# One accumulating DMA in place of four matrix products: the softmax denominators of a fused attention and feed-forward kernel

## The reference, cut to what matters

```python
def _L0_xattn_ref(q, k, v):                      # q = layernorm(x), k = v = ctx
    qh = q.reshape(b * h, d // h, m)             # 8 heads of 32 rows, m = 512
    kh = k.reshape(b * h, d // h, -1)
    vh = v.reshape(b * h, c // h, -1)
    qk = jnp.einsum('bdm,bdn->bmn', qh, kh) * scale
    sm = jax.nn.softmax(qk, axis=-1)             # over n = 512
    ret = jnp.einsum('bmn,bcn->bcm', sm, vh)
x = x + _L0_xattn_ref(_layernorm(x), ctx_2048, ctx_2048)
x = x + _L0_ffn_ref(_layernorm(x), W1, W2)       # quantised activations and weights, silu
```

## Time and profile before

| | |
|---|---|
| median of 3 runs | 783.78 us (780.02 to 784.09) |
| span of the profiled execution, first to last instruction | 780.7 us |
| instructions | 13868 |
| DMA traffic | 76.66 MB, mean 98 GB/s |
| mean granted PE clock | 0.987 of full speed |

### The profile page before, as it was taken

One profiled execution on the slowest core, in us unless ns is written; L12 is line 12 of the kernel. 1 busy time (PEld: TensorE's weight loads), 2 busy tenths in 40 slices (PEclk: granted clock), 3 DMA queues, 4 the chain that ended last, 5 costly groups with the idle time before them and its releaser, 6 DMA issues.

```text
span 780.7 us, 13868 instructions
## 1 busy us (share of the span) xinstructions
PE 718.7 (92%) x4324; PEld 280.2 (36%) x4324; DVE 693.9 (89%) x1588; ACT 634.8 (81%) x1017; POOL 630.5 (81%) x627
## 2 busy tenths in 40 slices
PE   0578699999999999999999999999999999999984
PEld 0112243333444444333344444333334344433322
DVE  2779999999999999999999999999999999997552
ACT  5486788888888898888888889888888888888852
POOL 3764778888889888888888998888888889877761
PEclk9999699999999999999999999999999999999998
DMA  8673213444333443344433334333443334330100
GB/s 293 167 197 111 55 43 107 109 110 109 98 92 84 109 99 78 96 109 109 109 101 92 85 105 100 81 92 109 110 109 103 94 86 101 82 82 25 46 28 13
DMA packets 53960, 76.66 MB, mean 98 GB/s; under 512 B 7808, under 2 KB 32384, under 8 KB 52864
## 3 DMA queue, kind: packets, MB, share of 16 engines
q1 hardware_dynamic: 53888, 75.79, 37.0%
HBM read 41.94 MB, written 8.39 MB: 64 GB/s over the span
## 4 chain that ended last, share of the span: by engine, by line
PE 83%; DVE 8%; DMA 3%; issue 2%; ACT 2%; SPq 1%; POOL 1%; POOLq 0%; ACTq 0%; DVEq 0%
PE pv L912 15%; PE mxp L902 15%; PE st L892 14%; PE bank_b L943 14%; PE dn L921 7%; PE bank_a L972 7%; PE bank_b L972 7%; DVE mx L727 4%; PE bank_a L931 3%; DMA late<-w 1%; DMA qs<-ql 1%; DMA qs<-qh 1%; ACT probs L585 1%; DVE late L796 1%; PE bank_a L954 1%
## 5 line engine op out<-in xcount | busy, mean ns | idle before, releaser
L585 ACT ACTIVATE probs<-st,sm 128x512 f32<-128x512 f32 x512 | 336.6, 687 | 52.7 <-PE st L892 26.9
L503 POOL TENSOR_TENSOR sums<-probs 128x512 f32<-128x512 f32 x256 | 333.3, 1321 | 20.8 <-ACT probs L585 20.8
L727 DVE TENSOR_REDUCE mx<-mxp 128x1 f32<-128x512 f32 x512 | 332.8, 676 | 18.5 <-PE mxp L902 14.9
L902 PE MATMUL mxp<-ks,qs 96*128 96x512 f16 x512 | 191.0, 403 | 18.2 <-DVE mx L727 12.4
L892 PE MATMUL st<-qs,ks 98*128 98x512 f16 x512 | 200.8, 394 | 1.7 <-ACT probs L585 1.6
L943 PE MATMUL bank_b<-w2t,late 128*128 128x512 f16 x512 | 128.1, 383 | 3.0 <-ACT late L615 3.0
L912 PE MATMUL pv<-probs,vt 128*32 128x512 f32 x1024 | 124.0, 602 | 0.0
L495 POOL TENSOR_TENSOR ql<-xn,qh 128x512 f16<-128x512 f32 x32 | 37.2, 1164 | 67.2 <-ACT qh L606 67.2
L892 PEld LDWEIGHTS st<-qs,ks 98*128 98x128 f16 x512 | 52.8, 103 | 99.3 <-ACT probs L585 40.1
L902 PEld LDWEIGHTS mxp<-ks,qs 96*128 96x128 f16 x512 | 50.7, 99 | 103.3 <-DVE mx L727 78.6
L801 DVE TENSOR_REDUCE hmx<-late 128x1 f32<-128x512 f32 x128 | 84.3, 679 | 1.1
(11 more groups left out here) (79 smaller groups left out, 896.6 us busy)
## 6 DMA issues: line engine op xcount, KB each, us to landing
cs<-ctx SPq DMA_DIRECT2D x32, 256.0 KB, 4.2
xs<-x SPq DMA_DIRECT2D x32, 256.0 KB, 4.0
late<-w SPq DMA_DIRECT2D x8, 1024.0 KB, 9.2
ks<-kh SPq DMA_DIRECT2D x64, 128.0 KB, 3.2
qs<-qh SPq DMA_DIRECT2D x64, 128.0 KB, 3.6
xr<-x SPq DMA_DIRECT2D x32, 256.0 KB, 3.0
vt<-values_t SPq DMA_DIRECT2D x32, 256.0 KB, 2.9
out<-late SPq DMA_DIRECT2D x32, 256.0 KB, 2.0
```

The source lines that it names most:

```text
L503: pool.tensor_tensor(sums[:, pair, h, :], probs[:, 2 * pair, h, :], probs[:, 2 * pair + 1, h, :], ALU.add).then_inc(sum_done, 1)
L585: act.activation(probs[:, c, h, :], st[u % 2][:, :], ACT.Exp, scale=sm1[:, r, ESC:ESC + 1]).then_inc(exp_done, 1)
L727: dve.reduce_max(mx[:, slot.ring(off), NC * h + c:NC * h + c + 1], mxp[m % 2][:, :], axis=AX.X).then_inc(max_done, 1)
L902: pe.matmul(mxp[m % 2][:, :], qs[0:3 * DH, r, h, c * P:(c + 1) * P], ks[0:3 * DH, r, h, :], start=True, stop=True).then_inc(mx_done, 1)
```

## The change

One step, `fold`, is added on POOL at unit 13: a DMA that adds all of `sums[:, 1]` into `sums[:, 0]` (float32, 128 partitions x 8 KB, 1 MB), issued by POOL once all eight sums are done, and it counts on a semaphore of its own when it has landed. `denominators` becomes one step of four products on `sums[:, 0]`, at 18 instead of two at 17, and waits for that semaphore. `invert` moves from 17 to 18. The first sum of pair 0 and of pair 1 now both wait for the one `denominators` of the tile before.

```diff
     sums=[4, 8, 9, 9, 10, 11, 11, 12],
-    denominators=[17, 17],
-    invert=[17],
+    fold=[13],
+    denominators=[18],
+    invert=[18],
...
-ORDER = {'pool': ['hidden_quantise', 'quantise', 'sums', 'xn', 'residual', 'rstd', 'ql', 'finish', 'rstd2', 'xn2',
+ORDER = {'pool': ['hidden_quantise', 'quantise', 'sums', 'fold', 'xn', 'residual', 'rstd', 'ql', 'finish', 'rstd2', 'xn2',
...
                 if h == 0:
-                    wait(pool, dn_done, slot, 2, off - 1, pair + 1)
+                    wait(pool, dn_done, slot, 1, off - 1, 1)
...
+            def fold(slot, off):
+
+                wait(pool, sum_done, slot, 2 * TH, off, 2 * TH)
+                pool.dma_start(sums[:, 0, :, :], sums[:, 1, :, :], accum_op=ALU.add).then_inc(sum_folded, 16)
...
-                wait(dve, dn_done, slot, 2, off, 2)
+                wait(dve, dn_done, slot, 1, off, 1)
...
-            def denominators(slot, off, pair):
-                wait(pe, sum_done, slot, 2 * TH, off, TH * (pair + 1))
-                if pair == 0:
-                    wait(pe, dn_spread, slot, 1, off - 1, 1)
+            def denominators(slot, off):
+                wait(pe, sum_folded, slot, 16, off, 16)
+                wait(pe, dn_spread, slot, 1, off - 1, 1)
                 for h in range(TH):
-                    last = pe.matmul(dn[DH * h:DH * (h + 1), :], ones[:, 0:DH], sums[:, pair, h, :],
-                                     start=(pair == 0), stop=(pair == 1), skip_group_check=True)
+                    last = pe.matmul(dn[DH * h:DH * (h + 1), :], ones[:, 0:DH], sums[:, 0, h, :],
+                                     start=True, stop=True, skip_group_check=True)
                 last.then_inc(dn_done, 1)
```

More of the change, by code:

```diff
@@ L315, in build @@
         sum_done = sem("sum_done")
+        sum_folded = sem("sum_folded")
         dn_done = sem("dn_done")
@@ L560, in run @@
                          "key_rsqrt": key_rsqrt, "xn": normalise, "ql": query_low, "finish": finish,
-                         "sums": pair_sum}
+                         "sums": pair_sum, "fold": fold}
                 for u in range(UNITS):
```

## The result

The changed kernel takes 1083.82 us (median of 4 runs, 1081.02 to 1085.94) against 783.75 us before: ratio 1.385, 95% interval 1.381 to 1.389. Forecast were 1140 us with a range of 950 to 1300.

A forecast was written before the change was run, and what follows sets the result against it. Bound: a closed loop from POOL's last sum through PE's denominators to the next tile's sums. Per tile 9.5 (landing) - 1.0 (removed) + 3.0 (clock) = +11.5 us; 31 intervals give +356 on 783.8, 1140 us, range 950 to 1300.

The forecast's parts named there:

- The closed loop: POOL's last sum, PE's denominators and the next tile's sums form a loop as long as the period, 0.4 us spare.
- D, the fold's landing: Time from POOL's last sum to the fold's landing, all added to the loop: 9.5 us, between 5.9 and 15.3.
- The prediction's own sign for the landing: The profile after would show a 1024 KB DMA from POOL with a landing of 8 to 10 us.
- What goes out of the loop: One product set (0.45 us) and work moved ahead of PE's wait (0.58 us) leave the loop: -1.0 us a tile.
- The first set costs and gives nothing: Dropping PE's first four denominator products, 0.9 us a tile, gains nothing: they covered a wait for unit 0's exponential.
- The clock: PE's stall halves its clock for about 6 us of work in each tile: +3.0 us, ends 0 and +6.5.
- The rival in which the clock stays: PE keeps full speed between stalls: landing still 9.5 us, +8.5 us a tile, 1047 us; chance 0.10.
- The rival of the plain rate: The fold lands like a plain transfer, in 5.9 us: 936 us, or 1029 with the clock loss; chance 0.22.
- The slow accumulate: The fold lands as late as the slowest weight load or later: 15.3 us, +17.3 a tile, 1320 us; chance 0.17.
- The other side: Not slower: the fold lands before PE reaches the denominators, below 1.1 us; at best 755 us, rather 780; chance 0.02.
- POOL's issue: Issuing the fold holds POOL 0.35 to 0.65 us, perhaps more; counted in the landing, later POOL work covered by idle time.

The follow-up runs named there:

- no_fold17: The changed kernel without the accumulating DMA (pair 1 missing from the denominators), its one set of denominator products and invert at 17 instead of 18; 779.9 us, ratio 0.997.
- plain_copy: The changed kernel with the same DMA as a plain copy, without the addition, so the denominators hold pair 1 alone; 984.1 us.
- keep_clock: The changed kernel with 26 extra PE products (about 5.5 us) ahead of the wait for the fold, to fill the stall; 1029.2 us, ratio 1.316.
- no_fold: The changed kernel without the accumulating DMA, one set of denominator products still at 18, pair 1 missing from them; 799.7 us, ratio 1.022.
- beside_store: The kernel before plus an accumulating DMA into a spare buffer no product reads, and SP's store moved from 56 to 61; 782.35 us, ratio 1.0005.
- beside: The kernel before, both product sets kept, plus the same accumulating DMA into a spare buffer that no product reads or waits for; 817.8 us, ratio 1.047.
- after_store: The changed kernel with SP's store moved from 56 to 61, so copies of kh and kl go ahead of it; 1081.7 us, ratio 1.383.

## Why the prediction was right, step by step

**The closed loop** was right, and it is what made the forecast. The sum by tiles: 300 us over 32 tiles are 9.4 us a tile (11.5 forecast, and over 31 intervals; the first tile's fold delays it too, 77.9 us for its first denominator against 69.5). One reading under it was wrong: the 57 waits of the earlier trace rows are the weight load's, not those of PE's matmuls, which never idled there. Before the change PE's own work held the period, with the loop over the last sum right behind it (`no_fold17`). The sum is not touched by this, since it counts from the last sum's end to the next scores as measured, 1.30 us, and the transfer makes that loop the longer one by far.

**D, the fold's landing** was sized too long: 7.5 us from the last sum in 24 tiles, 9.3 in the other eight, 8.0 on average against 9.5. The working that counted reading twice at the rate of 365 GB/s gave 7.7. I moved it up to 9.5 for SP's copies beside it and for the 9.2 us of the weight loads; but the usual landing is 7.1 to 7.2 us with these copies beside it, and they are the ones that suffer: `out` lands 5.7 us after its issue instead of 2.0. The prediction's own sign for the landing, 8 to 10 us, was missed with it, and the stall in front of `dn` is 6.5 us, not near 8. This is the term that accounts for most of the 56 us between forecast and result: 1.5 x 31 = 47 us. The clock's 0.5 x 31 = 16 us come on top, and the first tile's 8 us, which the sum did not have, go the other way. That D = 7.7 had been priced at 1084 us, the time measured, is partly luck: these two cancel most of each other.

The Trainium skill's rule that an add costs a second read through the same ring (page "Collectives: The Full Stack", section "The bandwidth ceiling: the fold count and why AG ≠ RS ≠ AR") fits: 0.645 against 0.33 us a packet. The runs show the halved rate; that the second read is its cause is the page's reason, which no run here isolates. Its plain figure of 2.0 us and 436 GB/s ("DMA: Bandwidth & Descriptors", section "Anatomy of one DMA — SWDGE (gpsimd) path") gives an estimate of 4.4 us for 1 MB; `plain_copy` had 4.7. With the bytes doubled, that estimate of 6.8 us is closer to the measured 7.2 than my 9.5 was.

**What goes out of the loop**, -1.0 us: right. With D = 7.47 and no clock loss `keep_clock` has a period of 28.23 us, 21.66 + 7.47 - 0.90; the 0.90 is what is left over.

**The first set costs and gives nothing**: right, 2 us by `no_fold17`. But the sentence that a fold taking no time would leave the period as it is was not quite: PE arrives 1.43 us after the sum, not 1.1, and 0.55 us a tile is lost at 18 (`no_fold`, 17.5 us). It did not enter the sum, in which D is far longer.

**The clock**: the term was right in kind, 2.5 us measured against 3.0. The granted clock is 0.5 for 5.4 us behind the stall of the period above, where I had read 6 from the two cases of before. The rival in which the clock stays is refuted.

**The rival of the plain rate** is refuted for the accumulating DMA (landing 7.1 us at least, not 5.9), and holds for a plain one, which at 4.7 us is faster still. **The slow accumulate** is refuted: 9.3 us at most, not 15.3. **The other side** had its turning point at 1.1 us; no version came near it, and `no_fold` shows that even zero would not have been faster at 18.

**POOL's issue** is 0.93 us, longer than SP's 0.35 to 0.65, and free: in `beside_store` it costs nothing.

What the prediction lacked is the price that the transfer puts on others: 35 us in `beside`, hidden in the changed kernel by the stall itself: the order that won the 35 us back in `beside_store` is worth 2 us in `after_store`. Whoever takes the stall away has to take this away too.

## What to carry to other kernels

Before swapping engine work for a DMA, find the loop that sets the period and ask whether the DMA's landing lies in it: some 27 us of a busy engine were worth 2 us here, and a landing of 7.2 us cost 6.6 us in each tile (7.5 from the last sum, less the 0.9 that went out of the loop), plus 2.5 us for the clock that the stall let fall. Count an accumulating transfer as it was measured here, at half the rate of a plain one plus 2 us, and cut it into pieces that start with their data: two halves won 54 us. And look at what the issuing queues send in the same moment: one due time on SP decided between 35 us and nothing.

## What the hardware showed that I had not expected

- One accumulating transfer of 1 MB takes 5.2 us of packets on 16 engines (eight of 0.645 us on each) and 2.0 us besides; a plain one 2.7 us of packets. POOL is held 0.93 us by the first and 0.63 us by the second.
- With the fold in flight SP's issue of two copies takes 2.6 us instead of 1.3, and their landing 6.2 us instead of 3.2 (`ks<-kh` in `beside`).
- The fold lands 8.4 to 9.3 us after its issue in eight tiles of the changed kernel, in the first and in seven in a row between 292 and 496 us. In all eight a 16 KB packet of the instruction queue falls between issue and landing; in none of the other 24 does one. One such fold, the DMA queues between 421.5 and 432.5 us:

```profile
q8 instruction: 1, 0.02, 0.5%
...
sums<-sums POOLq DMA_DIRECT2D x1, 1024.0 KB, 9.2
```

  The kernel needs about one such packet a tile. In this run the two go together in all 32 tiles, but the packet is neither needed for a late landing nor enough for one. The first tile has another reason: POOL is held 2.1 us by that issue instead of 0.93, and in `beside` the first transfer lands after 8.6 us without such a packet. The issue in the changed kernel (ns min/median/max), and a packet beside a transfer of usual landing in `beside_store`, between 619.5 and 626.8 us:

```profile
L511 POOL DMA_DIRECT2D sums<-sums x32: 922/926/2122, 69.2 to 1041.2; - x32
...
q8 instruction: 1, 0.02, 1.0%
...
spare<-sums POOLq DMA_DIRECT2D x1, 1024.0 KB, 7.2
```

  In `beside_store` ten such packets begin between issue and landing, and three of these transfers land after 7.1 to 7.2 us all the same. The three packets begin within 0.3 us of the issue and are over before the transfer's own first packets, which start 1.5 us after it. So the packet's place against the fold may decide over 2 us; this is seen side by side only, no run moved that packet alone, and it stays open.
